# Two pairs instead of four tiles in the DMA-accumulated part of a CIN layer, and small matmuls laid in row and column groups

## The chip, the cores and the metric

One Trainium2 chip, one of its cores. The time is that of one execution of the program on the device, in microseconds (us), the median of several runs. TensorE is written PE, its weight loads PEld, VectorE DVE, ScalarE ACT, GpSimd POOL and SyncE SP.

## The reference

1,024 examples, each with 32 categorical fields. Every field looks up a row of 32 numbers in its own table, which gives x of shape (1024, 32 fields, 32 numbers). Three layers of a compressed interaction network follow, and a small MLP on their sums:

```python
z0 = relu(einsum('bhd,bmd,ohm->bod', x, x, W0) + b0)    # 128 outputs; 64 go on as h1, 64 are "direct"
z1 = relu(einsum('bhd,bmd,ohm->bod', h1, x, W1) + b1)   # 128 outputs; 64 go on as h2, 64 are "direct"
z2 = relu(einsum('bhd,bmd,ohm->bod', h2, x, W2) + b2)   # 1 output
z = concat([z0[:, 64:], z1[:, 64:], z2], axis=1).sum(-1) # 129 numbers an example
h = relu(concat([z, dense_ctx]) @ W_top1 + b_top1)       # 145 -> 512
y = relu(h @ W_top2 + b_top2) @ W_top3                   # 512 -> 256 -> 1
```

All of it is float32, and the results must hold to float32-like accuracy.

## The kernel before

**Chunks.** The 1024 x 32 columns (example, number) are cut into 32 chunks of 1024 columns. The partitions hold pairs of fields: `x_base` holds each field four times (four "quads"), `x_roll[b]`, b = 0 to 3, the field that the pair's other side has, and `h_roll[a]`, a = 0 to 3, the 64 rows of h1 twice, rotated by 16a partitions. A layer is an elementwise product on DVE, [128 x 1024] for one tile, and a matmul against the weights for that tile, accumulated in PSUM. Layer 0 of a chunk takes 4 such tiles in two pairs (`products0`, `layer0`) and a small rest for fields that lie 16 apart: one product of [128 x 256] (`product16`) against four weight tiles, `layer0_pairs16` (L693), into `z0_ps`. Layer 1 takes 16 tiles into `z1_ps`.

**Three ways to feed layer 1.** Six tiles ("whole", in three pairs) go to PE as float32. Six ("split", in three pairs) go as fp32r in three passes: DVE makes the product `raw`, ACT rounds it to `prod_hi`, DVE subtracts to `prod_lo` (`split_rest`), and PE does w_hi by hi, w_hi by lo and w_lo by hi. Four tiles ("added") go in three passes too, but their low part is made without DVE: DVE writes `raw_add` (L529), ACT writes the rounded `add_hi` and the negative of it, `add_lo` (L881; L887 multiplies by -1), and POOL issues a DMA that adds `raw_add` onto `add_lo` in SBUF, 512 KB (L310 to L314). `raw_add`, `add_hi` and `add_lo` are rings of two tiles. PE's `added` (L680) waits for that transfer before its first pass.

**Layer 2.** `layer2_u` (L703) multiplies `h2` by W2: two float32 matmuls with 128 x 128 weights and 256 columns into `u_ps`; DVE multiplies by x (`layer2`, L537), and after every fourth chunk `layer2_sum` (L712) sums over the fields, in four matmuls with weights of 32 columns, each into partitions 32u to 32u+31 of `z2_ps`.

**Order.** Every engine runs its own `step(c, u, group)` 32 times, in an order written out by hand; waits are on semaphores. PE in step c: layer 0 and pairs16 of chunk c+1, `layer2_u` of c-1, then for chunk c: added 0, whole 0, split 0, added 1, whole 1, split 1, added 2, whole 2, split 2, added 3 (L721). DVE and ACT work up to a step ahead (L560, L896). ACT's `relu0` (L838) evacuates `z0_ps`, first two halves into `h_roll[0]`, then the direct half. When the first two are written, SP issues six transfers that make the rolled copies (`roll_h`, L389, 1.5 MB in all), then the load of `x_roll[1]` of chunk c+2, and the other loads and the store of gathered rows around them (L404). POOL issues eight indirect gathers of table rows for chunk c+3, in groups of 3, 3 and 2 between the four `add_raw` (L316), and in one step of four first adds row numbers (`make_rows`, L296).

Every matmul is recorded under line L646 of a helper; which it is shows in its operands. `u_ps<-h,w_sb` is `layer2_u`, `z_ps<-hi,w_sb` and `z_ps<-lo,w_sb` are pairs16, `z_ps<-h2x,quad_ones` is `layer2_sum`, `z_ps<-add_hi` and `z_ps<-add_lo` are the added tiles, and `z_ps<-prod,w_sb` the float32 ones. A float32 matmul is recorded as two instructions.

Of the kernel before, what the change touches and what calls it, by code (L numbers as in the profile page):

```python
# [27 lines left out]
ALU = mybir.AluOpType  # L28
# [20 lines left out]
ADDED1 = 4  # L49
# [3 lines left out]
ADD_RING = 2  # L53
# [41 lines left out]

assert WHOLE1 * PAIR + SPLIT1 * PAIR + ADDED1 == ROLLS * ROLLS
assert UNROLL * SPLIT1 % SPLIT_RING == 0 and ADDED1 % ADD_RING == 0


def build_tower(nc, gather_ids, row_base, table, w0, w0_swapped, w1_whole, w1_split, w2, b0, b1, b2,  # L100
                dense_t, wt1a, wt1b, bt1, wt2, bt2, wt3, out):
    with ExitStack() as ctx:
# [16 lines left out]
        w16_sb = sb("w16_sb", [P, QUADS, P], F32R)  # L119
        w1_sb = sb("w1_sb", [P, WHOLE1 * PAIR, P])  # L120
        w1_hi = sb("w1_hi", [P, SPLIT1 * PAIR + ADDED1, P], F32R)
        w1_lo = sb("w1_lo", [P, SPLIT1 * PAIR + ADDED1, P], F32R)
        w2_sb = sb("w2_sb", [P, 2, P])
# [39 lines left out]
        w0_swap, w16_raw, w16_swap, w16_rest = [early[:, 4 * k:4 * (k + 1), :] for k in range(4)]  # L163
        w1_raw = early[:, 16:16 + SPLIT1 * PAIR + ADDED1, :]
# [60 lines left out]
        add_lo_ready = [sem(f"add_lo_ready{k}") for k in range(ADD_RING)]  # L225
# [58 lines left out]
        def _(pool):  # L284
# [25 lines left out]
            def add_raw(k, ready):  # L310
                pool.wait_ge(ids_loaded, 32)
                pool.wait_ge(minus_hi_ready, ready)
                nc.gpsimd.dma_start(add_lo[:, k % ADD_RING, :], raw_add[:, k % ADD_RING, :], accum_op=ALU.add  # L313
                                    ).then_inc(add_lo_ready[k % ADD_RING], 16)  # L314

            def step(c, u, group):  # L316
# [5 lines left out]
                add_raw(0, ready[0])  # L322
                if ahead:
                    if u == 1:
                        make_rows(group + 1)
                    gather((u + 3) % UNROLL, made, freed, range(0, 3))
                add_raw(1, ready[1])
                if ahead:
                    gather((u + 3) % UNROLL, made, freed, range(3, 6))
                add_raw(2, ready[2])  # L330
                if ahead:
                    gather((u + 3) % UNROLL, made, freed, range(6, GATHERS))
                add_raw(3, ready[3])
# [7 lines left out]
        def _(sp):  # L341
            def store_x(c, s):
# [20 lines left out]
            def load_part16(c, s):  # L363
                if not_first(c, 2):
                    sp.wait_ge(raw16_ready, c - 1)
                src = bass.AP(x_dram.tensor, c * (2 * FIELDS * CHUNK) + FIELDS // 2 * CHUNK,
                              [[CHUNK, FIELDS], [PART, QUADS], [1, PART]])
# [15 lines left out]
            def load_part(c, s):  # L383

                wait(sp, h2x_ready, c)
                src = bass.AP(x_dram.tensor, c * (2 * FIELDS * CHUNK), [[CHUNK, FIELDS], [PART, QUADS], [1, PART]])
                sp.dma_start(x_part[:, :], src).then_inc(x_part_loaded, 16)
# [40 lines left out]
            sp.dma_start(quad_ones[:, :], bass.AP(eye_dram.tensor, 0, [[0, FIELDS], [FIELDS, QUADS], [1, FIELDS]])  # L428
# [25 lines left out]
        def _(dve):  # L454
# [105 lines left out]
            def step(c, u, group):  # L560
# [8 lines left out]
                dve.wait_ge(h1_ready, 2 * (c + 1))  # L569
                add_product(c, u, 0)  # L570
# [5 lines left out]

                dve.wait_ge(h1_rolled[s][0], (c - s + 2) * 16)
                add_product(c, u, 1)
# [5 lines left out]
                split_rest(c, u, 0)  # L584
                split_product(c, u, 1)
# [3 lines left out]
                add_product(c, u, 2)  # L589
# [5 lines left out]
                add_product(c, u, 3)  # L595
# [5 lines left out]
            dve.wait_ge(w16_rest_placed, 16)  # L601
# [445 lines left out]
```

## Time and profile before

| | |
|---|---|
| median of 3 runs | 1182.15 us |
| the runs | 1185.72, 1166.99, 1182.15 us |
| the profiled execution | 1173.95 us, of which the profile spans 1172.0 us |
| PE busy | 1110.5 us (95%) |
| DVE busy | 1018.1 us (87%) |
| ACT busy | 651.8 us (56%) |
| POOL busy | 571.5 us (49%) |
| DMA | 226.27 MB moved, mean 193 GB/s |
| mean granted TensorE clock | 0.987 of full speed |

The profile is of one execution. A row of its page or of a view gives times in us from the start of the span unless it says ns. In a group of instructions the output stands left of the arrow, the inputs right of it; "<-" behind an idle time names what ended it.

### The profile page before, as it was taken

The page shows a single profiled execution, that of the slowest core. Times are in us where ns is not written, and L with a number is a line of the kernel's source. Part 1 is how long each engine was busy: PE and PEld are TensorE (multiplying, and loading weights), DVE is VectorE, ACT ScalarE, POOL GpSimd, SP SyncE. Part 2 cuts the span into 40 slices and gives each one's busy share as a digit, 9 for nine tenths or more (in the row PEclk, how much of TensorE's full clock was granted, in tenths as well). Part 3 has the DMA queues.
Part 4 walks back from the last instruction along what each step waited for, and adds up shares of the span by engine and source line. Part 5 has one row for each costly group of instructions (what it writes and reads, how often), then busy time and mean ns, then how long its engine had stood idle before and what let it go on. Part 6 is the DMA issues. An engine that isn't in the chain of part 4 may idle for free.

```text
span 1172.0 us, 12206 instructions
## 1 busy us (share of the span) xinstructions
PE 1110.5 (95%) x3736; PEld 679.4 (58%) x3736; DVE 1018.1 (87%) x636; ACT 651.8 (56%) x607; POOL 571.5 (49%) x398
## 2 busy tenths in 40 slices
PE   0799999999998999999999989999998999999998
PEld 0356666565665666666665656656565566565664
DVE  2699999999998899999999979999997999999863
ACT  0355565656565555655666546565554565656544
POOL 5555555554457454545554555554555555520100
PEclk9899999999998999999999999999998999999999
DMA  6788877788877678878777787877777777786730
GB/s 200 212 218 217 217 192 208 199 214 219 210 206 178 177 203 219 215 199 220 195 201 199 186 219 199 217 187 196 201 205 194 205 189 201 207 208 166 166 59 0
DMA packets 86455, 226.27 MB, mean 193 GB/s; under 512 B 15313, under 2 KB 36050, under 8 KB 86434
## 3 DMA queue, kind: packets, MB, share of 16 engines
q1 hardware_dynamic: 57602, 152.23, 41.1%
q0 software_dynamic: 26624, 71.33, 32.6%
q10 hardware_dynamic: 2208, 2.45, 0.7%
q8 instruction: 11, 0.18, 0.1%
q14 instruction: 10, 0.08, 0.0%
HBM read 99.98 MB, written 8.39 MB: 92 GB/s over the span
## 4 chain that ended last, share of the span: by engine, by line
PE 58%; DMA 18%; ACT 9%; issue 7%; POOL 4%; DVE 2%; SPq 1%; ACTq 0%; DVEq 0%; POOLq 0%
PE z_ps L646 57%; DMA add_lo<-raw_add 15%; POOL gathered L305 3%; ACT prod_hi L879 3%; DMA x_roll<-x_dram 2%; ACT h_roll L847 2%; ACT add_lo L887 2%; ACT add_hi L886 1%; ACT direct L851 1%; DVE prod L473 1%; PE mlp_ps L646 1%; PE u_ps L646 1%; POOL rows_sb L296 1%; DVE raw_add L534 1%; DVE prod_lo L526 0%
## 5 line engine op out<-in xcount | busy, mean ns | idle before, releaser
L646 PE MATMUL z_ps<-prod,w_sb 128*128 128x512 f32 x1280 | 579.5, 600 | 33.8 <-DVE prod L605 27.6
L305 POOL DMA_INDIRECT gathered<-in_table,rows_sb x256 | 433.6, 1694 | 136.0 <-issue 69.7
L646 PEld LDWEIGHTS z_ps<-prod,w_sb 128*128 128x128 f32 x1280 | 246.7, 193 | 296.5 <-issue 284.7
L313 POOL DMA_DIRECT2D add_lo<-raw_add x128 | 121.8, 951 | 422.2 <-ACT add_lo L887 417.3
L526 DVE TENSOR_TENSOR prod_lo<-raw,prod_hi 128x2048 fp32r<-128x2048 f32 x96 | 219.5, 2286 | 58.8 <-ACT prod_hi L879 58.8
L886 ACT CAST add_hi<-raw_add 128x1024 fp32r<-128x1024 f32 x128 | 134.0, 1047 | 191.7 <-DVE raw_add L534 159.5
L879 ACT CAST prod_hi<-raw 128x2048 fp32r<-128x2048 f32 x96 | 182.6, 1902 | 96.8 <-DVE raw L519 96.1
L519 DVE TENSOR_TENSOR raw<-h_roll,x_roll 128x2048 f32<-128x2048 f32 x96 | 219.8, 2290 | 2.2
L473 DVE TENSOR_TENSOR prod<-h_roll,x_roll 128x2048 f32<-128x2048 f32 x96 | 219.1, 2283 | 0.0
L473 DVE TENSOR_TENSOR prod<-x_base,x_roll 128x2048 f32<-128x2048 f32 x63 | 144.2, 2289 | 36.1 <-PE z_ps L646 20.8
L646 PE MATMUL z_ps<-prod_hi,w_hi 128*128 128x512 f32 x392 | 162.5, 494 | 0.0
L534 DVE TENSOR_TENSOR raw_add<-h_roll,x_roll 128x1024 f32<-128x1024 f32 x128 | 155.8, 1218 | 2.8 <-DMA add_lo<-raw_add 2.8
L887 ACT ACTIVATE add_lo<-raw_add 128x1024 fp32r<-128x1024 f32 x128 | 134.9, 1054 | 0.0
L847 ACT ACTIVATE h_roll<-z_ps,b_sb 64x1024 f32<-64x1024 f32 x64 | 71.1, 1110 | 104.1 <-PE z_ps L646 102.8
L646 PE MATMUL z_ps<-prod_lo,w_hi 128*128 128x512 f32 x392 | 124.2, 396 | 0.0
L646 PE MATMUL z_ps<-prod_hi,w_lo 128*128 128x512 f32 x392 | 123.6, 395 | 0.0
L646 PE MATMUL z_ps<-add_hi,w_hi 128*128 128x512 f32 x256 | 91.2, 438 | 19.5 <-DMA add_lo<-raw_add 19.3
L646 PEld LDWEIGHTS z_ps<-prod_hi,w_hi 128*128 128x128 f32 x392 | 74.0, 189 | 54.8 <-issue 45.9
L646 PEld LDWEIGHTS z_ps<-prod_hi,w_lo 128*128 128x128 f32 x392 | 73.5, 188 | 18.2
L646 PEld LDWEIGHTS z_ps<-prod_lo,w_hi 128*128 128x128 f32 x392 | 73.6, 188 | 18.0
L646 PE MATMUL z_ps<-add_hi,w_lo 128*128 128x512 f32 x256 | 82.2, 403 | 0.0
L646 PE MATMUL z_ps<-add_lo,w_hi 128*128 128x512 f32 x256 | 81.8, 401 | 0.0
(66 smaller groups left out, 634.3 us busy)
## 6 DMA issues: line engine op xcount, KB each, us to landing
x_roll<-x_dram SPq DMA_DIRECT2D x128, 512.0 KB, 6.5
add_lo<-raw_add POOLq DMA_DIRECT2D x128, 512.0 KB
x_base<-x_dram SPq DMA_DIRECT2D x32, 512.0 KB
h_roll<-h_roll SPq DMA_DIRECT2D x32, 448.0 KB
h_roll<-h_roll SPq DMA_DIRECT2D x32, 384.0 KB, 4.6
h_roll<-h_roll SPq DMA_DIRECT2D x32, 320.0 KB
x_dram<-gathered SPq DMA_DIRECT2D x64, 128.0 KB, 4.6
x_part<-x_dram SPq DMA_DIRECT2D x64, 128.0 KB, 8.1
```

The lines of the kernel that those rows point to most:

```text
L296: nc.gpsimd.tensor_tensor(rows_sb[:, :], ids_sb[:, bass.ds(group * cols, cols)], base_sb[:, :], ALU.add).then_inc(rows_made, 1)
L305: nc.gpsimd.indirect_dma_start(gathered[:, u % 2, g * DIM:(g + 1) * DIM], None, table, bass.IndirectOffsetOnAxis(ap=rows_sb[:, col:col + 1 ...
L313: nc.gpsimd.dma_start(add_lo[:, k % ADD_RING, :], raw_add[:, k % ADD_RING, :], accum_op=ALU.add).then_inc(add_lo_ready[k % ADD_RING], 16)
L473: nc.vector.tensor_tensor(prod[:, slot, :, :], in0, in1, ALU.mult).then_inc(prod_ready, 1)
L519: nc.vector.tensor_tensor(raw[:, :, :], h_roll[:, s, PAIR:2 * PAIR, :], twice(x_roll[:, s, b, :]), ALU.mult).then_inc(raw_ready, 1)
L526: nc.vector.tensor_tensor(prod_lo[:, slot, :, :], raw[:, :, :], prod_hi[:, slot, :, :], ALU.subtract).then_inc(lo_ready, 1)
L534: nc.vector.tensor_tensor(raw_add[:, k % ADD_RING, :], h_roll[:, s, k, :], x_roll[:, s, ROLLS - 1, :], ALU.mult).then_inc(raw_add_ready, 1)
L646: return nc.tensor.matmul(*args, **kw)
L847: nc.scalar.activation(h_roll[half * HID:(half + 1) * HID, s, 0, :], z0_ps[0:HID, :], ACT.Relu, bias=b0_sb[0:HID, :]).then_inc(h1_ready, 1)
L879: nc.scalar.copy(prod_hi[:, (u * SPLIT1 + b) % SPLIT_RING, :, :], raw[:, :, :]).then_inc(hi_ready, 1)
L886: nc.scalar.copy(add_hi[:, k % ADD_RING, :], raw_add[:, k % ADD_RING, :])
L887: nc.scalar.mul(add_lo[:, k % ADD_RING, :], raw_add[:, k % ADD_RING, :], -1.0).then_inc(minus_hi_ready, 1)
```

## The change

The four added tiles become two pairs: one product of [128 x 2048] each, one ACT pass of that width for each of `add_lo` and `add_hi` (now `add_lo` first), one accumulating transfer of 1 MB, and one buffer of one pair in place of the rings of two. PE's `added` first does the four matmuls by `w1_lo` and the four by `w1_hi` that read `add_hi` alone, and waits for the transfer only before the last four. The order of a step is changed on all engines: on PE added 0, whole 0, split 0, whole 1, split 1, added 1, whole 2, split 2; on ACT `relu0` is cut in two, and its direct half moves behind the next two rounding steps; on POOL the gathers go in two groups of four.

Pairs16 now has the partitions ordered by quad first and field second, so that each half of the partitions holds two quads. Each matmul takes 64 rows and 128 columns of weights, the halves by turns into the two banks of `z0_ps`; their number stays eight. `layer2_u` becomes four matmuls of 128 rows and 32 columns, each into its own 32 partitions of `u_ps`. The gathered rows, `x_part`, `x_part16` and `quad_ones` follow the new order of partitions.

```diff
-ADDED1 = 4
+ADDED1 = 2
-ADD_RING = 2
...
-        raw_add = sb("raw_add", [P, ADD_RING, CHUNK])
-        add_hi = sb("add_hi", [P, ADD_RING, CHUNK], F32R)
-        add_lo = sb("add_lo", [P, ADD_RING, CHUNK], F32R)
+        raw_add = sb("raw_add", [P, PAIR, CHUNK])
+        add_hi = sb("add_hi", [P, PAIR, CHUNK], F32R)
+        add_lo = sb("add_lo", [P, PAIR, CHUNK], F32R)
...
                 pool.wait_ge(minus_hi_ready, ready)
-                nc.gpsimd.dma_start(add_lo[:, k % ADD_RING, :], raw_add[:, k % ADD_RING, :], accum_op=ALU.add
-                                    ).then_inc(add_lo_ready[k % ADD_RING], 16)
+                nc.gpsimd.dma_start(add_lo[:, :, :], raw_add[:, :, :], accum_op=ALU.add
+                                    ).then_inc(add_lo_ready, 16)
...
                 for copy in range(2):
                     to = bass.AP(x_dram.tensor, at + copy * (FIELDS * CHUNK),
-                                 [[CHUNK, FIELDS], [PART, QUADS], [1, PART]])
+                                 [[PART, QUADS], [CHUNK, FIELDS], [1, PART]])
...
             def add_product(c, u, k):
                 s = u % 2
 
-                if k >= ADD_RING or not_first(c):
-                    dve.wait_ge(add_lo_ready[k % ADD_RING], 16 * (c * (ADDED1 // ADD_RING) + k // ADD_RING))
-                nc.vector.tensor_tensor(raw_add[:, k % ADD_RING, :], h_roll[:, s, k, :], x_roll[:, s, ROLLS - 1, :],
+                if k > 0 or not_first(c):
+                    dve.wait_ge(add_hi_ready, c * ADDED1 + k)
+                    dve.wait_ge(add_lo_ready, 16 * (c * ADDED1 + k))
+                nc.vector.tensor_tensor(raw_add[:, :, :], h_roll[:, s, k * PAIR:(k + 1) * PAIR, :],
+                                        twice(x_roll[:, s, ROLLS - 1, :]),
                                         ALU.mult).then_inc(raw_add_ready, 1)
...
                 dve.wait_ge(h1_ready, 2 * (c + 1))
+                dve.wait_ge(h1_rolled[s][0], (c - s + 2) * 16)
                 add_product(c, u, 0)
...
-                add_product(c, u, 1)
                 products1(c, u, 0)
...
                 split_rest(c, u, 0)
+                add_product(c, u, 1)
                 split_product(c, u, 1)
...
                 products1(c, u, 1)
-                add_product(c, u, 2)
...
                 products1(c, u, 2)
-                add_product(c, u, 3)
...
             def added(c, k):
 
-                pe.wait_ge(add_lo_ready[k % ADD_RING], 16 * (c * (ADDED1 // ADD_RING) + k // ADD_RING + 1))
-                three_passes(z1_ps, SPLIT1 * PAIR + k, add_hi[:, k % ADD_RING, :], add_lo[:, k % ADD_RING, :],
-                             start=k == 0, stop=k == ADDED1 - 1).then_inc(add_used, 1)
+                pe.wait_ge(add_hi_ready, c * ADDED1 + k + 1)
+                for a in range(PAIR):
+                    t = (SPLIT1 + k) * PAIR + a
+                    over_banks(z1_ps, w1_lo[:, t, :], add_hi[:, a, :], start=k == 0 and a == 0)
+                    over_banks(z1_ps, w1_hi[:, t, :], add_hi[:, a, :])
+
+                pe.wait_ge(add_lo_ready, 16 * (c * ADDED1 + k + 1))
+                for a in range(PAIR):
+                    last = over_banks(z1_ps, w1_hi[:, (SPLIT1 + k) * PAIR + a, :], add_lo[:, a, :])
+                last.then_inc(add_used, 1)
...
-                for q in range(QUADS):
-                    cols = slice(q * PART, (q + 1) * PART)
-                    mm(z0_ps[:, cols], w16_sb[:, q, :], hi16[:, :], start=False, stop=False)
-                    last = mm(z0_ps[:, cols], w16_sb[:, q, :], lo16[:, :], start=False,
-                              stop=(q + 1) * PART % BANK == 0)
+                for t in range(PAIR):
+                    for part in (hi16, lo16):
+                        for half in range(PAIR):
+                            q = PAIR * half + t
+                            rows = slice(half * HID, (half + 1) * HID)
+                            last = mm(z0_ps[:, q * PART:(q + 1) * PART], w16_sb[rows, t, :], part[rows, :],
+                                      start=False, stop=t == PAIR - 1 and part is lo16)
...
-                for t in range(2):
-                    last = mm(u_ps[:, :], w2_sb[:, t, :], h2[:, t * PART:(t + 1) * PART],
-                              start=t == 0, stop=t == 1)
+                for q in range(QUADS):
+                    half, t = divmod(q, PAIR)
+                    last = mm(u_ps[FIELDS * q:FIELDS * (q + 1), :], w2_sb[:, half, :],
+                              h2[:, t * PART:(t + 1) * PART], start=True, stop=True)
...
                 split(c, u, 0)
-                added(c, 1)
                 whole1(c, 1)
                 split(c, u, 1)
-                added(c, 2)
+                added(c, 1)
                 whole1(c, 2)
-                split(c, u, 2)
                 if u == 0 and not_first(c):
                     layer2_sum(c, group - 1)
-                added(c, 3)
+                split(c, u, 2)
...
                 act.wait_ge(raw_add_ready, c * ADDED1 + k + 1)
-                if k >= ADD_RING or not_first(c):
-                    act.wait_ge(add_used, c * ADDED1 + k + 1 - ADD_RING)
-                nc.scalar.copy(add_hi[:, k % ADD_RING, :], raw_add[:, k % ADD_RING, :])
-                nc.scalar.mul(add_lo[:, k % ADD_RING, :], raw_add[:, k % ADD_RING, :], -1.0
+                if k > 0 or not_first(c):
+                    act.wait_ge(add_used, c * ADDED1 + k)
+                nc.scalar.mul(add_lo[:, :, :], raw_add[:, :, :], -1.0
                               ).then_inc(minus_hi_ready, 1)
+                nc.scalar.copy(add_hi[:, :, :], raw_add[:, :, :]).then_inc(add_hi_ready, 1)
...
                     relu1(c - 1, (u - 1) % UNROLL)
...
-                    round_added(c, 1)
...
-                    relu0(c + 1, (u + 1) % UNROLL)
+                    relu0_h(c + 1, (u + 1) % UNROLL)
+                round_added(c, 1)
                 round_products(c, u, 1)
-                round_added(c, 2)
+                if not is_last(c):
+                    relu0_direct(c + 1, (u + 1) % UNROLL)
                 round_products(c, u, 2)
-                round_added(c, 3)
```

## Rows read from the trace of the kernel before

**Rows 1.** The page: busy time of each engine.
```profile
PE 1110.5 (95%) x3736; PEld 679.4 (58%) x3736; DVE 1018.1 (87%) x636; ACT 651.8 (56%) x607; POOL 571.5 (49%) x398
```

**Rows 2.** Waits of PE (engine, line, releaser: us in total, times, longest).
```profile
PE z_ps L646 <- DMA add_lo<-raw_add: 19.3, 19, 4.1
```

**Rows 3.** Timeline of ACT: relu0 of chunks 2 and 31 (start, length).
```profile
95.04 1.11 ACT L847 ACTIVATE h_roll<-z_ps,b_sb 64x1024 f32<-64x1024 f32 x1 [3.27 <-PE z_ps L646]
...
1086.95 2.25 ACT L847 ACTIVATE h_roll<-z_ps,b_sb 64x1024 f32<-64x1024 f32 x2 [3.27 <-PE z_ps L646]
```

**Rows 4.** Timeline of PE over one step, 569 to 604 us.
```profile
569.53 0.29 PE L646 MATMUL z_ps<-lo,w_sb 128*128 128x256 f32 x1
569.65 1.03 PE L646 MATMUL u_ps<-h,w_sb 128*128 128x256 f32 x4
...
570.99 0.62 PE L646 MATMUL z_ps<-add_lo,w_hi 128*128 128x512 f32 x2
571.91 3.60 PE L646 MATMUL z_ps<-prod,w_sb 128*128 128x512 f32 x8
...
578.15 0.62 PE L646 MATMUL z_ps<-add_hi,w_hi 128*128 128x512 f32 x2
...
586.12 0.73 PE L646 MATMUL z_ps<-add_hi,w_hi 128*128 128x512 f32 x2 [0.18 <-DMA add_lo<-raw_add]
...
603.08 1.03 PE L646 MATMUL u_ps<-h,w_sb 128*128 128x256 f32 x4
```

**Rows 5.** Timeline of PE around layer2_sum.
```profile
626.91 0.63 PE L646 MATMUL z_ps<-prod_hi,w_lo 128*128 128x512 f32 x2
627.47 0.64 PE L646 MATMUL z_ps<-h2x,quad_ones 128*32 128x256 f32 x8
628.04 0.73 PE L646 MATMUL z_ps<-add_hi,w_hi 128*128 128x512 f32 x2
628.61 0.63 PE L646 MATMUL z_ps<-add_lo,w_hi 128*128 128x512 f32 x2
```

**Rows 6.** Timeline of POOL, ACT and PE in a long step, 351 to 403 us.
```profile
351.03 7.45 POOL L296 TENSOR_TENSOR rows_sb<-ids_sb,base_sb 128x32 int32<-128x32 int32 x1
...
362.73 2.25 ACT L847 ACTIVATE h_roll<-z_ps,b_sb 64x1024 f32<-64x1024 f32 x2 [3.04 <-PE z_ps L646]
...
366.15 1.01 POOL L313 DMA_DIRECT2D add_lo<-raw_add  x1
...
374.87 1.22 PE L646 MATMUL z_ps<-add_hi,w_hi 128*128 128x512 f32 x2 [3.81 <-DMA add_lo<-raw_add]
...
402.22 1.11 ACT L847 ACTIVATE h_roll<-z_ps,b_sb 64x1024 f32<-64x1024 f32 x1 [3.41 <-PE z_ps L646]
```

**Rows 7.** The chain that ended last, in order of time, at 575 us.
```profile
576.25 0.97 ACT add_lo L887
...
577.77 8.31 DMA add_lo<-raw_add
```

**Rows 8.** DMA from 592 to 597.5 us, and SP's issues around it.
```profile
q0 software_dynamic: 144, 0.52, 55.3%
...
594.16 0.58 SPq L361 DMA_DIRECT2D x_base<-x_dram  x1
```

**Rows 9.** Timeline of POOL, gathers and the transfer after them.
```profile
592.18 0.88 POOL L313 DMA_DIRECT2D add_lo<-raw_add  x1 [5.30 <-ACT add_lo L887]
...
596.63 1.83 POOL L305 DMA_INDIRECT gathered<-in_table,rows_sb  x1 [0.30 <-issue]
```

**Rows 10.** Windows of 1 us: PE, PEld, DVE, ACT, POOL busy, clock, DMA share, GB/s.
```profile
596.00:597.00 1.00, 1.00 (x4) 0.40 (x3) 1.00 (x1) 0.95 (x3) 0.70 (x2) 1.00 0.77 242
```

**Rows 11.** Timeline of DVE and ACT: two 128x2048 products, one rounding.
```profile
544.48 2.29 DVE L519 TENSOR_TENSOR raw<-h_roll,x_roll 128x2048 f32<-128x2048 f32 x1
546.69 2.28 DVE L473 TENSOR_TENSOR prod<-h_roll,x_roll 128x2048 f32<-128x2048 f32 x1
...
573.40 1.90 ACT L879 CAST prod_hi<-raw 128x2048 fp32r<-128x2048 f32 x1
```

More of the change, by code:

```diff
@@ L162, in build_tower @@
         early = h_roll[:, 1, :, :].rearrange("p a (t n) -> p (a t) n", n=P)
-        w0_swap, w16_raw, w16_swap, w16_rest = [early[:, 4 * k:4 * (k + 1), :] for k in range(4)]
-        w1_raw = early[:, 16:16 + SPLIT1 * PAIR + ADDED1, :]
+        w0_swap = early[:, 0:ROLLS, :]
+        w16_raw, w16_swap, w16_rest = [early[:, ROLLS * k:ROLLS * k + PAIR, :] for k in range(1, 4)]
+        w1_raw = early[:, 16:16 + (SPLIT1 + ADDED1) * PAIR, :]
         mlp1 = h_roll[:, 0, :, :]
@@ L224, in build_tower @@
         minus_hi_ready = sem("minus_hi_ready")
-        add_lo_ready = [sem(f"add_lo_ready{k}") for k in range(ADD_RING)]
+        add_hi_ready = sem("add_hi_ready")
+        add_lo_ready = sem("add_lo_ready")
         add_used = sem("add_used")
@@ L322, in step @@
                 add_raw(0, ready[0])
+                if ahead and u == 1:
+                    make_rows(group + 1)
                 if ahead:
-                    if u == 1:
-                        make_rows(group + 1)
-                    gather((u + 3) % UNROLL, made, freed, range(0, 3))
+                    gather((u + 3) % UNROLL, made, freed, range(0, GATHERS // 2))
                 add_raw(1, ready[1])
                 if ahead:
[L329 to L333, printed above, removed]
+                    gather((u + 3) % UNROLL, made, freed, range(GATHERS // 2, GATHERS))
             make_rows(0)
@@ L921, in _ @@
             act.wait_ge(w16_rest_ready, 1)
-            act.dma_start(w16_raw[P // 2:P, :, :], w16_rest[P // 2:P, :, :]).then_inc(w16_rest_placed, 16)
+            for q in range(QUADS):
+                low_half = slice(FIELDS * q + FIELDS // 2, FIELDS * (q + 1))
+                act.dma_start(w16_raw[low_half, :, :], w16_rest[low_half, :, :]).then_inc(w16_rest_placed, 16)
             round_pairs16(0)
-            relu0(0, 0)
+            relu0_h(0, 0)
+            relu0_direct(0, 0)
             over_chunks(act, step)
@@ L994, in lay_out @@
     for q in range(QUADS):
-        for rows in (QUADS * low + q, QUADS * (low + FIELDS // 2) + q):
-            w0_tiles[rows, ROLLS + q, :] = w0[:, low, low + FIELDS // 2].T
-            w0_swapped[rows, ROLLS + q, :] = w0[:, low + FIELDS // 2, low].T
+        for rows in (FIELDS * q + low, FIELDS * q + low + FIELDS // 2):
+            w0_tiles[rows, ROLLS + q % PAIR, :] = w0[:, low, low + FIELDS // 2].T
+            w0_swapped[rows, ROLLS + q % PAIR, :] = w0[:, low + FIELDS // 2, low].T
     arrays["w0"], arrays["w0_swapped"] = w0_tiles, w0_swapped
@@ L1006, in lay_out @@
     arrays["w1_split"] = np.stack([w1_tile(b, k) for b in range(SPLIT1) for k in range(PAIR, ROLLS)]
-                                  + [w1_tile(ROLLS - 1, k) for k in range(ADDED1)], axis=1)
+                                  + [w1_tile(ROLLS - 1, k) for k in range(ADDED1 * PAIR)], axis=1)
     w2 = a["L0_rec_W2"].reshape(HID, FIELDS)
-    w2_tiles = np.zeros((P, 2, P), w2.dtype)
-    for q in range(QUADS):
-        half, t = divmod(q, 2)
-        w2_tiles[half * HID:(half + 1) * HID, t, q::QUADS] = w2
+    w2_tiles = np.zeros((P, PAIR, FIELDS), w2.dtype)
+    for half in range(PAIR):
+        w2_tiles[half * HID:(half + 1) * HID, half, :] = w2
     arrays["w2"] = w2_tiles
```

44 lines of the change are left out of this document (22 added, 22 removed).

## Prediction

> **What bounds the kernel now.** I read the page's busy times first: PE is busy 95% of the span, DVE 87% [rows 1], so a gain has to shorten PE's work or PE's waits. Then the waits: once it runs, PE waits for one thing only, the accumulating transfers, 19.3 us in 19 waits [rows 2]. Then a step's length. `relu0` follows the end of pairs16 at once, so its starts mark the steps: from chunk 2 to chunk 31, 95.04 to 1086.95 us, 29 steps of 34.2 us [rows 3]. Last the timeline of one step, from one `layer2_u` to the next: 569.65 to 603.08, 33.43 us [rows 4]. There added 2 starts at 586.12 instead of 585.79 (578.15 + three passes of a tile, 1.40, + whole and split, 571.91 to 578.15 = 6.24), and its first pair of matmuls takes 0.57 instead of 0.47, since the pipe has run empty. Without these 0.43 PE's own work is 33.0 us. `layer2_sum` costs 0.77 in every fourth step (below), 0.2 a step. So PE's work is 33.2 and waits make 1.0 a step, 29 us in all. Most of these sit in a few long steps: `make_rows` took 7.45 us at 351, `add_raw` 1 was issued only at 366.15 behind the gathers, PE waited 3.81 us, its next pair took 1.22 instead of 0.73, and the step, 362.73 to 402.22, took 39.5 us [rows 6].
>
> **PE's work after the change.** The three passes stay 24 matmuls for the four added tiles; their order costs nothing, as all rows of passes are evenly 0.47 a pair [rows 4]. Pairs16 is eight matmuls of 0.12 (the last starts at 569.53, its follower at 569.65), 0.94; `layer2_u` takes until the first added pair, 570.99 - 0.47 - 569.65 = 0.87 [rows 4]. Together 1.81.
>
> For groups of columns the trace has a case of the very same form as the new `layer2_u`, 128 x 32 weights and 256 columns, eight instructions: `layer2_sum`. The matmul before ends its stream at 626.91 + 0.47 = 627.38, the group starts at 627.47, the next pair at 628.04 takes 0.57 instead of 0.47: 628.61 - 627.38 - 0.47 = 0.77 [rows 5]. One after another eight instructions of 0.21 (0.87 / 4) would take 1.7, so the groups do run side by side, but on both sides the array empties, and the gain of `layer2_u` is 0.1 only. For groups of rows there is no row. If the halves run side by side, four times 0.12 = 0.47, and 0.16 until the last has left the array (the last one lasts 0.29, of which 0.12 is its stream). The sum for both is 0.09 + 0.63 + 0.57 + 0.10 = 1.40, a gain of 0.4 a step. Bounds: if nothing is lost at the borders, 0.47 + 0.43 = 0.90, a gain of 0.9; if the halves run one behind the other, 0.94 + 0.16 + 0.76 = 1.86, no gain. I take 0.4, as the row of the same form shows the borders' cost.
> The Trainium skill (TensorEngine Tiling (Array Packing), Key Properties) says that changing the tiling mode drains TensorE, and the new step goes from the full array to halves of rows, to quarters of columns and back. By that rule the trace agrees: 0.77 where 0.43 would do; a sum without the rule would gain 0.9 a step.
>
> New work of PE: 33.2 - 0.4 = 32.8 us a step.
>
> **The two transfers.** Let T be the start of `layer2_u`, T' the next, 32.8 later. A 512 KB transfer that meets no other is issued at 592.18 [rows 9], and its packets end, with the share of DMA falling, within the window to 597 [rows 10], by when `x_base`, issued at 594.16, has begun: at most 4.8 us. Its own packets are 55.3% of 5.5 us, 3.0 us on all 16 engines [rows 8]. Behind the rolled copies it takes 8.31 us [rows 7]. So the second 512 KB adds 3.0: 7.8 and 11.3; upper bounds are twice the rows, 9.6 and 16.6, the lower ones 7.4 (a start-up shared) and 8.31.
>
> *Second pair.* PE: 0.67 for `layer2_u`, added 0 until 3.5, whole and split 6.24 each, 15.9, eight matmuls of `add_hi` until 17.8, then it needs the low part. ACT: the one buffer frees at 3.5 + 0.2; the negation (1.9, as a rounding of that width [rows 11]) ends at 5.6, the issue follows 0.6 later (577.77 - 577.22 [rows 7]), at 6.2, and the transfer lands at 6.2 + 11.3 = 17.5. That is 0.3 in hand; at 16.6 it would be 5.0 late.
>
> *First pair.* ACT goes on with the copy and `prod_hi` 1 until 9.3; only then does DVE start the subtraction of split 1 and its next five passes, to the end of the new pair's product: 6 x 2.2 (546.69 - 544.48 [rows 11]) = 13.2, 22.5. Negation 24.5, issue 25.1, landed 32.9; PE needs it at T' + 0.67 + 1.87 = 35.3: 2.4 in hand. DVE's second pair product needs the buffer too: after four passes and two of 0.34, 9.5, at 32.0, so DVE waits 0.9. It has the time: its work is 13 passes of 2.2, 28.7, and 2.2 of small ones, 30.9 of 32.8. This closes a loop: 13.2, negation and issue 2.6, transfer D, then product, `raw` 1, sum, `prod` 1 and `layer2`, 8.1, together 23.9 + D: 31.7 at D = 7.8. It binds PE from D = 8.9 on.
>
> **POOL.** Gathers take 1.8 and a pause of 0.3 [rows 9]; four from T + 27.3 end at T' + 3, and the second pair's issue is wanted at T' + 5.6: 2.6 in hand. A POOL instruction 5 to 7 us too long now makes a step 6.3 us longer (39.5 - 33.2 [rows 6]); then it would make it about 3 longer, and too short a wait for the clock to fall.
>
> **Other edits.** DVE's four products of half width become two, as wide as the others; ACT's eight passes become four: both lie beside PE's work, and without that cover they are worth under 0.3. `relu0`'s direct half goes behind `prod_hi` 1: nobody waits for it before the next layer 0, at T + 25. Stores and loads with the new order of partitions move the same 1 KB pieces and are priced at nothing: what waits for the store first is `x_base`, issued at 594.16 [rows 8], more than 20 us ahead of its product. `x_roll[1]` queues behind 3 us more of traffic, and may hold DVE back by 0.8, which it has.
>
> **Sum.** With so little in hand I leave 0.3 a step for waits: 33.1. 29 x (34.2 - 33.1) = 32. The first step has a transfer of 3 us more before PE's first low pass, hidden in part by the high passes (+2), the last one no layer 0 to cover its first transfer (+1). 1173.95 - 32 + 3 = 1145. The median of before is 8 above its profiled run, and its runs spread over 19, which I put to more or fewer long steps; these get cheaper, so of the 8 I keep 3: 1148.
>
> **Rivals.**
> *Borders hidden* (0.9 gained): 29 x 0.5 less, 1133. Against it stands the 0.77 of `layer2_sum` [rows 5].
> *Halves of rows one behind the other:* 0.4 more a step, 1160. For it: no row shows them side by side. Against: columns do.
> *First pair cut in two by `x_base`:* SP issues that load when DVE's `prod` for it is done, now T + 27, inside the first pair's transfer (27 to 33). If the engines turn to it half way, its 512 KB add 3.0: D = 10.8, the loop takes 34.7, and the time is 1173.95 + 29 x 0.5 + 3 = 1191, no change that can be told. Now it comes as the 512 KB end [rows 8, 10]. The Trainium skill (DMA: Bandwidth & Descriptors, arbitration) says that each DMA engine turns round-robin between its queues a packet of descriptors at a time; by that rule this rival would come true, and the trace leaves it open.
> *The second pair comes late (slower than before):* behind the rolled copies, 1.5 MB, and with `x_roll[1]` beside it, its D may be nearer twice 8.31. PE then waits before the last four matmuls of added 1 in every step. From D = 13 the step is over 34.2 and the kernel slower; at 15 it is 3.4 late, 36.5 with the pipe's refill, 1173.95 + 29 x 2.3 + 3 = 1244. Against it: 8.31 holds one wait for the copies, which doesn't double.
>
> **Chances.** Forecast 0.45 (its own range 1136 to 1160), borders hidden 0.10, halves in a row 0.18, first pair cut 0.14, second pair late 0.13. The range 1128 to 1195 leaves out the last and a little of the second. About 2% is what a measurement of this kernel can tell: 1158.5 and 1205.8. Faster: 0.40 + 0.10 + 0.08 = 0.58; slower: 0.12; the rest, 0.30, within.
>
> **What would show it.** In the changed profile pairs16 and `layer2_u` should take 1.4 us together; PE's waits on `add_lo` should be short and at added 1; transfers of the second pair should land by T + 17.8; no step should exceed 37; DVE should wait about 1 us for `add_lo` before its second pair product. A step of 34.5 with DVE waiting 3 us for the first transfer speaks for the cut; one with PE idle 3 us before the last four matmuls of added 1 for the late pair. My forecast is wrong above all if either transfer takes 1.5 us more than reckoned.

## The result, and the profile after

The changed kernel takes 1194.04 us (median of 4 runs, 1184.27 to 1195.72), the kernel before 1174.57 beside it (4 runs, 1164.89 to 1185.72): a ratio of 1.0161 [1.0098, 1.0224]. Ratios here and below leave out runs more than 1.5% above the fastest run of their kernel, so they can differ by up to half a per cent from the quotient of the medians beside them. The forecast was 1148. The time is inside the forecast's range (1128 to 1195), at its upper end, but on the other side of no change.

The page of the changed kernel, its busy times:

```profile
PE 1103.6 (93%) x3864; PEld 644.9 (54%) x3864; DVE 1011.6 (85%) x572; ACT 627.6 (53%) x479; POOL 558.6 (47%) x334
```

Every engine is busy for less time than before [rows 1], and for a smaller share: work has gone, and waits have come. The waits of the changed kernel (engine, line, releaser: us in total, times, longest):

```profile
DVE prod L470 <- DMA x_roll<-x_dram: 58.9, 28, 5.6
...
DVE raw_add L532 <- DMA add_lo<-raw_add: 42.9, 32, 2.3
...
PE z_ps L642 <- DMA add_lo<-raw_add: 41.0, 27, 3.2
```

PE waits 41.0 us for the accumulating transfers, once in nearly every step (19.3 before [rows 2]); DVE waits 42.9 for them, and 58.9 for a plain load, `x_roll`. The same two in the kernel before:

```profile
DVE prod L473 <- DMA x_roll<-x_dram: 14.7, 11, 5.5
...
DVE raw_add L534 <- DMA add_lo<-raw_add: 2.8, 2, 2.6
```

The steps, by `relu0` of chunks 2 and 31 (timeline of ACT):

```profile
99.24 2.25 ACT L850 ACTIVATE h_roll<-z_ps,b_sb 64x1024 f32<-64x1024 f32 x2 [0.48 <-PE z_ps L642]
...
1103.40 2.25 ACT L850 ACTIVATE h_roll<-z_ps,b_sb 64x1024 f32<-64x1024 f32 x2 [1.50 <-PE z_ps L642]
```

Against [rows 3] the start is 4.2 us longer, each of the 29 steps takes 34.63 instead of 34.2 (12.3 in all), and what follows the last `relu0` is 3.0 longer (1191.5 - 1103.4 against 1172.0 - 1086.95). These make the 19.5 us between the two spans.

PE's own work did what was forecast. Its timeline over pairs16, `layer2_u` and the first added pair:

```profile
547.54 0.38 PE L642 MATMUL z_ps<-hi,w_sb 64*128 64x256 f32 x2
547.76 0.28 PE L642 MATMUL z_ps<-lo,w_sb 64*128 64x256 f32 x2
...
548.20 0.64 PE L642 MATMUL u_ps<-h,w_sb 128*32 128x256 f32 x8
548.77 0.73 PE L642 MATMUL z_ps<-add_hi,w_lo 128*128 128x512 f32 x2
549.34 0.63 PE L642 MATMUL z_ps<-add_hi,w_hi 128*128 128x512 f32 x2
```

Pairs16 takes 548.20 - 547.54 = 0.66 and `layer2_u` 0.57; with 0.09 ahead and 0.10 behind, as reckoned before, 1.42 us in place of 1.81. What sets the step shows in the chain of the changed kernel that ended last (start us, us, what); here it goes round without PE:

```profile
541.74 8.11 DMA add_lo<-raw_add
...
552.12 2.28 DVE raw L516
554.40 1.13 DVE top_a L548
555.53 2.21 DVE prod L470
...
557.91 11.12 DMA x_roll<-x_dram
...
571.42 2.30 DVE raw_add L532
573.74 1.93 ACT add_lo L892
...
576.22 8.25 DMA add_lo<-raw_add
```

One turn, 541.74 to 576.22, is 34.48 us: the first pair's transfer (8.1); DVE's second pair product and `raw` 1; the sum of the direct halves; `prod` of pair 1, which frees `x_roll[1]`; the load of `x_roll[1]` for the chunk after next (11.1); layer 0's product from it; the next first pair product, its negation and the issue. Loads and copies move as many bytes as before, but this load and the second pair's transfer take longer. I took each transfer's time from its issue to the last of its landings in the trace: the first pair's takes 8.2 us, the second pair's 12.6 on the median (half of them within 11.8 to 13.5), and PE waits 2.0 us for the latter, ahead of the last four matmuls of added 1 (timeline of PE):

```profile
568.18 1.20 PE L642 MATMUL z_ps<-add_lo,w_hi 128*128 128x512 f32 x4 [2.01 <-DMA add_lo<-raw_add]
```

The landings also told where to look. Before, each 128 KB store of gathered rows and each load of `x_part` and `x_part16` left 16; in the changed kernel each leaves 5, of which one comes with the issue. I read the other four as 4 DMA engines in place of 16; the rule at the end of this section and the runs below bear this out, no view names an engine. The landings of the loads beside them fit four engines with more to do: of the 16 landings of a load of `x_roll` the thirteenth comes 0.7 to 2.0 us after the twelfth (medians of its eight buffers), and 1.3 us after it in the second pair's transfer, where in the kernel before it comes at most 0.2 after. The start of the program shows what this does, as hardly anything else runs there. The windows of 1 us (PE, PEld, DVE, ACT, POOL busy, clock, DMA share of 16 engines, GB/s) around the first stores; the kernel before:

```profile
17.00:18.00 1.00, 0.00 (x0) 0.00 (x0) 0.00 (x0) 0.00 (x0) 0.69 (x2) 1.00 0.83 255
```

The changed kernel:

```profile
17.00:18.00 1.00, 0.00 (x0) 0.00 (x0) 0.00 (x0) 0.00 (x0) 0.75 (x1) 1.00 0.29 52
18.00:19.00 1.00, 0.00 (x0) 0.00 (x0) 0.00 (x0) 0.00 (x0) 0.69 (x2) 1.00 0.28 93
```

And SP's issues, where `x_base` waits for the two stores; before:

```profile
16.07 0.84 SPq L350 DMA_DIRECT2D x_dram<-gathered  x2
18.32 0.58 SPq L361 DMA_DIRECT2D x_base<-x_dram  x1
```

After:

```profile
15.90 1.18 SPq L347 DMA_DIRECT2D x_dram<-gathered  x2
21.56 0.65 SPq L358 DMA_DIRECT2D x_base<-x_dram  x1
```

Before, the DMA share reaches 0.83 for one microsecond; after, it stays between 0.16 and 0.38 from 17 to 21 us, and the first load comes 3.2 us later. The diff made the slowest dimension of these patterns in DRAM the quads, a dimension of 4, where it had been the fields, 32. The Trainium skill (DMA: Bandwidth & Descriptors, Why a DMA increments its semaphore by 16 and not by 1, "How many engines (k)") says that a DMA runs on the largest number of engines up to 16 that divides the slowest dimension of both its patterns, and that transfers issued by SP take the lowest-numbered ones; by that rule the trace agrees: 4 engines here, 16 before. Which four they are stands in no view of this case.

### The profile page after: what moved, and what is told of

The parts are those of the page before. It is cut to its first block, busy times and chain, and to the rows that moved or that the text cites. A ratio compares the mean times of both kernels' runs of the same rounds, so it can differ in the third digit from the quotient of the medians.

```text
span 1191.5 us, 12068 instructions
## 1 busy us (share of the span) xinstructions
PE 1103.6 (93%) x3864; PEld 644.9 (54%) x3864; DVE 1011.6 (85%) x572; ACT 627.6 (53%) x479; POOL 558.6 (47%) x334
## 3 DMA queue, kind: packets, MB, share of 16 engines
q0 software_dynamic: 17408, 71.32, 32.8%
## 4 chain that ended last, share of the span: by engine, by line
DMA 47%; DVE 20%; issue 12%; PE 11%; ACT 6%; POOL 2%; DVEq 1%; SPq 0%; POOLq 0%; ACTq 0%
DMA x_roll<-x_dram 23%; DMA add_lo<-raw_add 22%; PE z_ps L642 10%; DVE raw_add L532 6%; DVE prod L470 6%; DVE raw L516 5%; ACT add_lo L892 5%; DVE top_a L548 2%; POOL gathered L306 1%; DVE prod_lo L523 1%; DMA h_roll<-h_roll 1%; PE mlp_ps L642 1%; ACT prod_hi L885 1%; ACT add_hi L894 1%; DMA x_dram<-gathered 0%
## 5 line engine op out<-in xcount | busy, mean ns | idle before, releaser
L306 POOL DMA_INDIRECT gathered<-in_table,rows_sb x256 | 488.4, 1908 | 131.8 <-issue 68.6
L892 ACT ACTIVATE add_lo<-raw_add 128x2048 fp32r<-128x2048 f32 x64 | 122.5, 1914 | 330.5 <-DVE raw_add L532 301.6
L314 POOL DMA_DIRECT2D add_lo<-raw_add x64 | 62.0, 969 | 448.6 <-ACT add_lo L892 436.9
L470 DVE TENSOR_TENSOR prod<-x_base,x_roll 128x2048 f32<-128x2048 f32 x63 | 144.1, 2288 | 59.2 <-DMA x_roll<-x_dram 58.9
L532 DVE TENSOR_TENSOR raw_add<-h_roll,x_roll 128x2048 f32<-128x2048 f32 x64 | 146.6, 2291 | 45.5 <-DMA add_lo<-raw_add 42.9
L894 ACT CAST add_hi<-raw_add 128x2048 fp32r<-128x2048 f32 x64 | 120.6, 1884 | 0.0
L642 PE MATMUL z_ps<-add_lo,w_hi 128*128 128x512 f32 x256 | 74.7, 414 | 41.0 <-DMA add_lo<-raw_add 41.0
L642 PE MATMUL z_ps<-add_hi,w_lo 128*128 128x512 f32 x256 | 85.5, 415 | 0.0
L642 PE MATMUL z_ps<-add_hi,w_hi 128*128 128x512 f32 x256 | 82.2, 402 | 0.0
```

The source lines that it names most:

```text
L306: nc.gpsimd.indirect_dma_start(gathered[:, u % 2, g * DIM:(g + 1) * DIM], None, table, bass.IndirectOffsetOnAxis(ap=rows_sb[:, col:col + 1 ...
L314: nc.gpsimd.dma_start(add_lo[:, :, :], raw_add[:, :, :], accum_op=ALU.add).then_inc(add_lo_ready, 16)
L470: nc.vector.tensor_tensor(prod[:, slot, :, :], in0, in1, ALU.mult).then_inc(prod_ready, 1)
L532: nc.vector.tensor_tensor(raw_add[:, :, :], h_roll[:, s, k * PAIR:(k + 1) * PAIR, :], twice(x_roll[:, s, ROLLS - 1, :]), ALU.mult).then_in ...
L642: return nc.tensor.matmul(*args, **kw)
L892: nc.scalar.mul(add_lo[:, :, :], raw_add[:, :, :], -1.0).then_inc(minus_hi_ready, 1)
```

## The experiments

Medians are of several runs; each ratio is to runs of the kernel before on the same chip, whose median went from 1169.9 to 1177.4 us between the chips; kernels run on different chips are compared by their ratios. The step is the mean over 29 steps of the profiled run. "New order" below is the order of partitions, quad first.

### Which half of the change costs

**Groups only.** The kernel before with the small matmuls in groups and the new order; the tiles stay four.

```diff
...
-                    mm(z0_ps[:, cols], w16_sb[:, q, :], hi16[:, :], start=False, stop=False)
+                            rows = slice(half * HID, (half + 1) * HID)
+                            last = mm(z0_ps[:, q * PART:(q + 1) * PART], w16_sb[rows, t, :], part[rows, :],
...
-                    last = mm(u_ps[:, :], w2_sb[:, t, :], h2[:, t * PART:(t + 1) * PART],
+                    last = mm(u_ps[FIELDS * q:FIELDS * (q + 1), :], w2_sb[:, half, :],
...
```

> The kernel before with the row and column groups of pairs16 and layer2_u alone, the four added tiles as they were. The trace after shows both together at 1.43 us a step where before had 1.81. The kernel before is bound by PE, so if its steps shorten with PE's work: 29 x 0.4 = 12 us less than before, about 0.99 of it. Rival (the small matmuls or the new order of partitions cost the rise): same as before or above it.

1175.05 us, 1.0058 [1.0020, 1.0096]: no gain from PE's 0.4 us a step. The chain of this kernel goes round through the third transfer as well as PE:

```profile
543.64 8.38 DMA add_lo<-raw_add
552.07 16.85 PE z_ps L647 x56
...
576.86 8.62 DMA add_lo<-raw_add
585.53 16.85 PE z_ps L647 x56
```

PE's stretch of the turn is 16.85 us, and in the same stretch of the kernel before's chain 17.14: the gain of pairs16. The turn is still 33.46 us long, against 33.43 in [rows 4], because what lies between (`relu0`, three passes of ACT and the third transfer, here 8.62 against 8.31 in [rows 7]) took the 0.3 back, and the gain of `layer2_u` falls outside the turn. So where the kernel before goes round this way too, as in [rows 7], it is held by a loop through a transfer, and not by PE's work alone. The profiled run also starts late: `relu0` of chunk 2 comes at 100.8 instead of 95.0 us, which the new order alone does as well (below).

**Pairs only.** The changed kernel with the small matmuls on the full array as before, new order kept.

```diff
-                    last = mm(u_ps[FIELDS * q:FIELDS * (q + 1), :], w2_sb[:, half, :],
+                    last = mm(u_ps[:, :], w2_sb[:, t, :], h2[:, t * PART:(t + 1) * PART],
```

> The kernel after with pairs16 and layer2_u as full-array matmuls again, everything else as after. Loop theory: a loop without PE in it sets the step (second added product, raw 1, sum, prod 1, load of x_roll[1], first layer-0 product, first added product, negation, 1 MB transfer, 34.6 us), so 0.4 us more on PE cost nothing or little: within 5 us of after. PE theory (PE's work plus a fixed wait for the second transfer): 12 us slower than after.

1193.23 us, 1.0185 [1.0140, 1.0229], step 34.51: the whole loss without the groups. The chain of this kernel goes in part another way than that of the changed one, through the second pair's transfer and PE behind it:

```profile
140.24 12.94 DMA add_lo<-raw_add
153.22 15.25 PE z_ps L642 x48
```

So two ways round lie close together here, and only a run that takes one of them away can tell what the other costs.

**PE's order.** The changed kernel with one line of PE moved.

```diff
                 split(c, u, 1)
+                whole1(c, 2)
                 added(c, 1)
-                whole1(c, 2)
```

> The kernel after with PE taking whole 2 before added 1, so that the second transfer is wanted 3.4 us later and PE's wait of 2.0 us for it should go. Loop theory: PE is not in the loop that binds; the wait goes elsewhere on PE, and the time stays within 10 us of after. Rival (the late second pair sets the step): 29 x 1.9 = 55 us less, about 1140.

1197.84 us, 1.0226 [1.0168, 1.0285], step 34.60. PE's wait for the second pair is gone (1.8 us in all), and PE waits 40.1 us for DVE's `prod` instead. With a whole pair's time more for the second pair's transfer nothing is won, so that wait alone was not the cause; the chain goes round without PE, and most steps are even, 34.2 to 35.2.

**The loop through DVE.** On top of that, DVE makes `raw` 1 and `prod` 1 ahead of the second pair product, so that `x_roll[1]` is free one pass of 2.3 us sooner; ACT rounds `raw` 1 ahead of the second pair as well.

```diff
+                split_product(c, u, 1)
+                products1(c, u, 1)
                 add_product(c, u, 1)
-                split_product(c, u, 1)
...
-                products1(c, u, 1)
...
```

> The kernel after with DVE doing raw 1 and prod 1 before the second added product (ACT rounds raw 1 before it as well) and PE taking whole 2 before added 1. Loop theory: x_roll[1] is free about 3.5 us earlier, its load is issued right behind the rolled copies and ahead of the second 1 MB transfer, the loop opens, and PE's own 32.8 us become the step: 29 x (34.7 - 33.0) = 49 less than after, 1144. Rival (1 MB transfers are too slow wherever they stand, D above 11 for the first): within 15 us of after.

1185.28 us, 1.0102 [1.0067, 1.0136], step 34.43. Better than the changed kernel, far from the 1144 expected. The chain of this kernel:

```profile
546.42 14.39 DMA x_roll<-x_dram
```

The load is issued earlier and takes 14.4 us instead of 11.1: SP now issues it 0.9 us after the last of the rolled copies, where it had been 3.3. This is so in about every other chunk: there the load takes 11.6 to 16.8 us and the step up to 39.5; in the others it takes 6.4 to 9.8 and the step at most 34.2. So the mean step hardly fell, and the question was why the transfers are slow.

### Which transfers cost

**Pairs, old order.** The changed kernel with the old order of partitions, and with it the full-array small matmuls.

```diff
-    [[PART, QUADS], [CHUNK, FIELDS], [1, PART]]
+    [[CHUNK, FIELDS], [PART, QUADS], [1, PART]]
...
```

> The kernel after with the old order of partitions and full-array small matmuls: the pairs and the new order of work alone. In the trace after, each 128 KB store of gathered rows and load of x_part and x_part16 lands with 5 semaphore updates where before has 16, so they run over four DMA engines, and the last four of the updates of every other transfer come about 3 us after the rest. Four-engine theory: that lateness goes, the second 1 MB transfer lands 2.5 us and x_roll[1] 3 us earlier, the loop of 34.6 us falls under PE's 33.2 and the time to 1150 to 1165, below e2 by 30 or more. Order theory (the loop is made by the order of DVE and SP alone): 1180 to 1195, as e2.

1158.26 us, 0.9840 [0.9781, 0.9898], step 33.42; the second pair lands after 11.0 us, and the thirteenth landings of the loads come at most 0.2 us after the twelfth again. Its chain is PE alone for three steps:

```profile
565.17 32.12 PE z_ps L642 x108
598.15 32.88 PE z_ps L642 x116
```

**The new order alone**, in the kernel before, with nothing else of the change.

```diff
-    [[CHUNK, FIELDS], [PART, QUADS], [1, PART]]
+    [[PART, QUADS], [CHUNK, FIELDS], [1, PART]]
...
```

> The kernel before with the new order of partitions alone (full-array small matmuls, four tiles, old order of work). Four-engine theory: the start is 5 us later, and the steps wait longer for the third transfer and for x_roll: 8 to 15 us above before, and above e1 by the 0.3 us a step that the groups give. Order theory: as before.

1180.22 us, 1.0056 [1.0008, 1.0105], step 34.19; `relu0` of chunk 2 comes at 100.7 instead of 95.0. So the new order costs the kernel before its start and nothing measurable in its steps, less than the 8 to 15 us expected, and costs the pairs 1.1 us a step (34.51 against 33.42). In the kernel before some transfers do get slower, the fourth accumulating one 7.3 us instead of 5.8, but the third, which its chain goes through, does not: 8.4 against 8.3. The four kernels together: four tiles, old and new order, 1 and 1.0056; pairs, old and new order, 0.984 and 1.0185 (pairs only). The two edits do not add up: the slow transfers hurt where the loop that sets the step runs through them.

**Changed kernel, cut by quads.** Each small store and load becomes four transfers of 32 partitions, whose slowest dimension in DRAM is 32 again. Bytes, rows and places are those of the changed kernel.

```diff
-    sp.dma_start(x_part[:, :], src).then_inc(x_part_loaded, 16)
+    for q in range(QUADS):
+        src = bass.AP(x_dram.tensor, c * (2 * FIELDS * CHUNK) + q * PART, [[CHUNK, FIELDS], [1, PART]])
+        sp.dma_start(x_part[FIELDS * q:FIELDS * (q + 1), :], src).then_inc(x_part_loaded, 16)
...
```

> The kernel after with each 128 KB store and each load of x_part and x_part16 cut into four transfers of 32 partitions, whose slowest dimension is 32 and no longer 4. Four-engine theory: as e8 and 0.4 us a step better, if SP's nine to twelve further issues of 0.6 us hide: 1140 to 1165. Order theory: 1185 or more, SP being busier.

1152.2 us (6 runs, 1150.69 to 1156.48), 0.980 [0.975, 0.985], step 33.10, faster than both kernels. The start is not given back: SP takes 3.6 us to issue the eight stores, the first load comes as late as in the changed kernel (21.56), and `relu0` of chunk 2 at 102.3 us.

```profile
16.53 3.58 SPq L348 DMA_DIRECT2D x_dram<-gathered  x8
21.58 0.64 SPq L359 DMA_DIRECT2D x_base<-x_dram  x1
```

Quiet steps, from one `layer2_u` to the next on PE, take 32.6 us:

```profile
535.46 0.64 PE L645 MATMUL u_ps<-h,w_sb 128*32 128x256 f32 x8
568.07 0.64 PE L645 MATMUL u_ps<-h,w_sb 128*32 128x256 f32 x8
600.67 0.64 PE L645 MATMUL u_ps<-h,w_sb 128*32 128x256 f32 x8
```

With the full array and the old order (the timeline of PE in the pairs, old order) they take 33.0; the 0.4 between is the gain of the groups, as forecast:

```profile
531.17 1.03 PE L642 MATMUL u_ps<-h,w_sb 128*128 128x256 f32 x4
564.15 1.03 PE L642 MATMUL u_ps<-h,w_sb 128*128 128x256 f32 x4
597.13 1.03 PE L642 MATMUL u_ps<-h,w_sb 128*128 128x256 f32 x4
```

**Stores cut, or loads cut.** The same cut for the two stores alone (first edit), and for the loads of `x_part` and `x_part16` alone (second).

```diff
...
-    sp.dma_start(to, gathered[:, s, :]).then_inc(x_stored[s], 16)
...
+        sp.dma_start(to, gathered[FIELDS * q:FIELDS * (q + 1), s, :]).then_inc(x_stored[s], 16)
```

```diff
...
-    sp.dma_start(x_part16[:, s, :], src).then_inc(x_part16_loaded[s], 16)
...
+        sp.dma_start(x_part16[FIELDS * q:FIELDS * (q + 1), s, :], src).then_inc(x_part16_loaded[s], 16)
```

> The changed kernel (1194 us) with only the two stores of gathered rows cut into four transfers of 32 partitions each; the loads of x_part and x_part16 stay on few engines. It asks which of the four small transfers of a chunk does the harm. If each 128 KB on four engines harms alike, half of the 42 us comes back: about 1172. If the stores do it (they stand ahead of x_base and beside the rolled copies): 1155 to 1160. If the loads do it (x_part and x_part16 are issued beside x_roll[1] and the accumulating transfers): 1185 to 1192.

> The changed kernel (1194 us) with only the loads of x_part and x_part16 cut into four transfers of 32 partitions each; the two stores of gathered rows stay whole. With only the stores cut the time stayed at 1194.5, with both cut it was 1152.2. Theory: the two loads of 128 KB do the harm, since they are issued around x_roll[1] and the second pair's transfer: 1150 to 1156, the second pair lands after 11 us instead of 12.6 and x_roll[1]'s load takes 9.3 instead of 11.1 us. Rival: either half of the small transfers is enough to hold the loop up, and only cutting all of them frees it: 1175 or more.

Stores cut: 1194.49 us, 1.0188 [1.0111, 1.0264], step 34.58, nothing won. Loads cut: 1150.13 us, 0.9876 [0.9824, 0.9929], step 33.10. So the two loads carry the whole loss of the steps, and the late thirteenth landings stay with the stores cut (1.1 us or more after the twelfth) and go with the loads cut (0.2 or less). The chain with the stores cut:

```profile
561.43 11.30 DMA x_roll<-x_dram
```

with the loads cut:

```profile
570.64 9.39 DMA x_roll<-x_dram
```

With 9.4 in place of 11.1 the turn of 34.48 us becomes 32.8, nearly level with PE's own work. The second pair lands after 12.6 us with the stores cut and 11.1 with the loads cut. Which of the two loads counts for more was not tried.

**Groups only, and the new order alone, both cut by quads.** The same cut in the two kernels with four tiles.

> e1 (before with the row and column groups) with the same cut into four. Four-engine theory: what e1 lost comes back, 10 us below before (1163), as PE's work is 0.4 us a step less and the third transfer as early as before; at least 5 below e1. Order theory: as e1, 1175.

> The kernel before with nothing but the new order of partitions in its small stores and loads, each of them cut into four transfers of 32 partitions. The uncut one took 1180.2 us against 1175.8. Theory of the four engines: the cut spreads them over 16 engines again, so the time is that of the kernel before, ratio 0.998 to 1.002, and the start loses at most 1 to 2 us of its 5. Rival, the new order costs by its smaller runs in memory or by SyncE's issues whatever the engines: ratio 1.005 or more, and the first relu0 still starts near 100.7 instead of 95.

Groups: 1168.15 us, 0.9956 [0.9914, 0.9998]: half a per cent with the late start counted in, half of the 10 us expected. The new order alone: 1188.7 us, 1.0152 [1.0082, 1.0221], a miss, and the rival's "1.005 or more" is what came. The transfers did come back: the fourth accumulating one lands after 5.8 us (7.3 uncut, 5.8 in the kernel before), and quiet steps take 33.0 to 33.5. The start came back by a third only, `relu0` of chunk 2 at 98.6. And five steps took 38 to 40.5. One of them, by the timelines of POOL, ACT and PE:

```profile
570.99 5.99 POOL L305 DMA_INDIRECT gathered<-in_table,rows_sb  x1 [2.02 <-DVE raw L494]
...
579.56 2.25 ACT L850 ACTIVATE h_roll<-z_ps,b_sb 64x1024 f32<-64x1024 f32 x2 [3.40 <-PE z_ps L649]
...
591.19 0.87 PE L649 MATMUL z_ps<-add_hi,w_hi 128*128 128x512 f32 x2 [3.31 <-DMA add_lo<-raw_add]
...
617.72 2.25 ACT L850 ACTIVATE h_roll<-z_ps,b_sb 64x1024 f32<-64x1024 f32 x2 [3.32 <-PE z_ps L649]
```

A gather of 6.0 us instead of 1.9 delays the issue of the next accumulating transfer, and PE waits. Four of the five long steps follow such a gather by 8 to 9 us; the fifth is the first after the start. The kernel before has two such gathers and the long `make_rows` of [rows 6], so in the two profiled runs the start (3.6 us), the end (2.9) and the steps (3.0) make a difference of 9.6 us. That is a little over half of the loss in the medians; the rest is not in this trace, and neither is why the same cut with the groups stood 2.0% lower, where the groups' 0.4 us a step make 1.0%. Why the gathers grow, and whether SP's twelve more issues a chunk have a part in it, stays open. The run neither confirms nor refutes the four engines in a kernel with four tiles; for the pairs stand the two runs above.

**By quads with `prod` 1 first.** The cut changed kernel with the new order on DVE, ACT and PE shown above, to see whether the loop still costs anything once the transfers are quick.

```diff
+                split_product(c, u, 1)
+                products1(c, u, 1)
                 add_product(c, u, 1)
...
```

> The changed kernel with each 128 KB store or load of the new partition order cut into four transfers of 32 partitions (1152.2 us), and on top of it the other order on VectorE: the raw product and prod of pair 1 come before the second pair product, and TensorE does whole 2 before added 1. It asks whether the loop over the two accumulating transfers and x_roll[1] still costs anything once four engines no longer carry the small transfers. If that loop still binds in the steps of 33.1: prod of pair 1 comes 2.3 us earlier, so x_roll[1] is issued earlier, step 32.7, about 1140 us. If TensorE's own work (32.8 predicted) binds there: no change, 1150 to 1154. If the earlier x_roll[1] load collides with the second pair's transfer, as it did with the four engines loaded (14.4 us instead of 11.1): 1155 to 1160, and the load takes longer than in the kernel without the new order.

1168.54 us, 0.9961 [0.9916, 1.0006], 16 us above the kernel without the new order on DVE. Direction as the third theory said, size missed. A stretch of its chain:

```profile
427.49 6.31 DMA x_dram<-gathered
...
443.15 12.61 DMA x_roll<-x_dram
```

SP waits for a store before `x_base`, and behind that wait stand the rolled copies; the load of `x_roll[1]`, no longer spaced by DVE, follows them at once; in the four long steps behind the start, 37 to 39 us, it takes 11.2 to 13.5 us where it took 9.4. Half of the steps take 32.6.

## Why the prediction was wrong

**The step that failed** is "stores and loads with the new order of partitions move the same 1 KB pieces and are priced at nothing". The pieces are the same; the engines that carry them are not. The changed kernel takes 1.6% longer than the kernel before; with every small transfer cut it takes 2.0% less (0.980), with the loads alone cut 1.2% less (0.9876). I looked at who waits for these transfers first, not at who shares engines with them. Nobody waits for `x_part`; `x_roll[1]` and the second pair wait behind it.

**The second step** is `x_roll[1]` "may hold DVE back by 0.8, which it has". It held DVE back by 2.1 a time (58.9 us, 28 times). And slack counted for DVE alone is not there to be spent: this load lies in a loop with the first pair's transfer. I had the loop of 23.9 + D, and "It binds PE from D = 8.9 on", but closed it along DVE's own passes alone, where it leaves DVE behind `prod` 1 and comes back by the load. The loop that was there is 15.2 us of DVE, ACT and issues, plus 8.2 and 11.1: 34.5. With the load at 9.4 it is 32.8, the same as the forecast of PE's work, so even the faster kernels have hardly any slack in it.

**Mis-sized.** The second pair was forecast to take 11.3 and took 12.6 in the changed kernel, 11.0 to 11.1 in those with quick loads, so the working was right for the transfers that it assumed. The first pair: 8.2 against 7.8. The start cost 4.2 instead of 2, the end 3.0 instead of 1. Waits of 0.3 a step became 1.8 (34.63 against 32.8); with the cut the step was 33.10, and forecast 33.1. A wait that makes the step about 3 us longer was called too short for the clock to fall. In the changed kernel's steps the granted clock fell to its lower level, 1.2 GHz, behind waits of PE of 1.8 to 2.2 us in five places, as here behind one of 1.83 us that ended at 430.91 (a window as above, of 4 us; the clock is the third number from its end):

```profile
431.00:435.00 4.00, 4.00 (x8) 2.30 (x9) 3.10 (x2) 0.00 (x0) 0.00 (x0) 0.57 0.63 195
```

Other waits of that length passed without a fall.

**Right.** Groups of rows and of columns run side by side and the borders cost what `layer2_sum` showed [rows 5]: 1.42 us against 1.40, a gain of 0.4 a step. The pairs gave POOL the room that [rows 6] lacked: gathers of 4.9 us lengthened no step of the cut kernel beyond 34.7. In the changed kernel two steps passed the bound of 37 that was given, with 37.2 and 37.5, and no such gather ahead of them. The pairs alone are worth 1.6% (old order), more than the groups.

**The rivals.** "Borders hidden" and "halves one behind the other" are out by the 1.42. "First pair cut by `x_base`": in the changed kernel that load was issued at 578.24, two microseconds into the first pair's transfer, which still took 8.25. So sharing the engines with it cost at most 0.45 us over the 7.8 reckoned, not 3.0. "The second pair comes late": it came 12.6 us after its issue on the median, short of the 13 from which that rival was to decide, but beyond 13 in 11 of 32 steps. PE waited 1.5 a time, half of what its sign asked, and moving PE's work in front of the wait won nothing. So its direction was right and its mechanism at most a part: with its wait gone, the loop with `x_roll[1]` set the same step.

**Luck.** That the time lies in the range says nothing for the working. The range reached up to 1195 for "first pair cut", reckoned at 1191, which did not happen.

## What to carry to other kernels

When an edit reorders partitions or dimensions, look at the outermost dimension of every DMA pattern that it touches, in DRAM too, and count the landings of one transfer: same bytes and same pieces do not mean same engines. A small transfer that nobody waits for can still set the time, through the transfers that share its engines, and most where the step is a loop through two or more transfers. To price a later landing, follow the whole loop back to itself before calling the slack of one engine enough.

## What the hardware showed unexpectedly

- Two loads of 128 KB a chunk on 4 DMA engines instead of 16 made a 512 KB load beside them take 10.7 to 11.3 us instead of 9.4, and a 1 MB accumulating transfer 12.6 instead of 11.0 (medians). In the kernel with four tiles, whose chain goes through a transfer that they did not slow (8.4 against 8.3), the same loads cost nothing measurable in the steps (34.19 against 34.2).
- A load issued right behind other transfers, about 2 us earlier than before, took 11.6 to 16.8 us in about every other chunk, instead of about 11, and 6.4 to 9.8 in the others.
- A gather on POOL, 1.7 to 1.9 us on the mean, takes much longer one to seven times an execution: 6.0 us in the kernels with four tiles, 4.9 in those with pairs. With four short transfers a step each of the 14 in five profiled runs stood 8 to 9 us ahead of a step 3 to 7 us too long; with two long transfers and the loads quick, six of them in one execution lengthened no step beyond 34.7.
